# Edge layers of a graph network: adding the gates in the gathers instead of on the vector engine

## The reference, cut to what matters

```
ea = silu(edge_attr @ We + be)              # the gates, once: 100000 x 128
for l in range(4):
    msg = relu(x[src] + ea)                 # gather a row for each edge, add its gate, clip at zero
    agg = segment_sum(msg, dst, num_segments=n)
    h = x + agg
    h = silu(h @ W1[l] + b1[l]) @ W2[l] + b2[l]
    y = x + h
    x = layernorm(y) * gamma[l] + beta[l]
```

## Time and profile before

| | |
|---|---|
| median of 3 runs | 9549.08 us (9542.76 to 9550.45) |
| the profiled execution, its own time | 9545.06 us |
| its span, first to last instruction | 9543.3 us |
| GpSimd busy | 6696.7 us, 70% |
| TensorE busy | 4661.5 us, 49% |
| VectorE busy | 4305.5 us, 45% |
| ScalarE busy | 529.1 us, 6% |
| granted TensorE clock, mean | 0.61 of full speed |
| DMA | 960.76 MB, 101 GB/s over the span |

### The profile page before, as it was taken

How to read it: one execution, slowest core, us unless ns; L and a number is a source line. 1 busy time by engine, 2 the same in 40 slices (tenths; PEclk the granted TensorE clock), 3 DMA queues, 4 the chain that set the end, 5 groups by cost and what they waited for, 6 DMA issues and landing times.

```text
span 9543.3 us, 143586 instructions
## 1 busy us (share of the span) xinstructions
PE 4661.5 (49%) x19975; PEld 3800.2 (40%) x19976; DVE 4305.5 (45%) x9490; ACT 529.1 (6%) x1108; POOL 6696.7 (70%) x6591
## 2 busy tenths in 40 slices
PE   2766735544455344544445444453455444544455
PEld 1444424433344333433334333343444334443444
DVE  3455565654566445654456445672223223332222
ACT  1222211100000000000000000000000000000000
POOL 1777626557777677767777677776777677767776
PEclk9577768865566556565556555665555555555566
DMA  3998854223333333333333333331222222222222
GB/s 102 262 271 263 249 153 128 83 77 98 99 101 101 88 98 102 100 89 98 98 100 101 87 97 99 99 90 45 54 54 57 51 53 56 55 51 53 54 58 53
DMA packets 907432, 960.76 MB, mean 101 GB/s; under 512 B 442719, under 2 KB 610042, under 8 KB 906872
## 3 DMA queue, kind: packets, MB, share of 16 engines
q0 software_dynamic: 213248, 462.82, 18.9%
q1 hardware_dynamic: 572380, 399.74, 15.4%
q10 hardware_dynamic: 121756, 97.77, 3.1%
HBM read 801.39 MB, written 164.71 MB: 101 GB/s over the span
## 4 chain that ended last, share of the span: by engine, by line
POOL 55%; issue 21%; DMA 9%; DVE 6%; PE 4%; DVEq 2%; POOLq 1%; ACTq 1%; SPq 1%; ACT 0%
POOL rows L693 52%; DMA gates_by_edge<-gate 7%; PE ps_seg L823 2%; POOL msg L713 1%; POOL sums L693 1%; POOLq L324 1%; DVE msg L1452 1%; PE ps_mm L847 1%; DMA rows<-node_rows,idx 0%; DMA kv_rows<-gate 0%; PE ps_big L878 0%; PE ps_t L835 0%; ACTq L368 0%; DVE group_stats L1355 0%; DVEq L1288 0%
## 5 line engine op out<-in xcount | busy, mean ns | idle before, releaser
L693 POOL DMA_INDIRECT rows<-node_rows,idx x5488 | 5573.0, 1015 | 1919.1 <-issue 1669.6
L823 PE MATMUL ps_seg<-msg,onehot 128*128 128x128 f32 (+1 forms) x9800 | 2142.0, 387 | 2553.1 <-DVE sums L1309 2274.6
L823 PEld LDWEIGHTS ps_seg<-msg,onehot 128*128 128x128 f32 x9800 | 1838.0, 279 | 2854.2 <-DVE sums L1309 2535.0
L1288 DVE SCALAR_TENSOR_TENSOR onehot<-iota_f,win_base,dst_ch 128x512 f32<-128x512 f32 x1968 | 1512.9, 769 | 3200.4 <-PE ps_seg L823 2554.6
L823 PE MATMUL ps_seg<-rows,onehot 128*128 x5880 | 1393.7, 417 | 1559.9 <-SPq L590 1450.7
L823 PEld LDWEIGHTS ps_seg<-rows,onehot 128*128 128x128 f32 x5880 | 1220.9, 310 | 1729.8 <-issue 1728.2
L1452 DVE TENSOR_TENSOR msg<-q_res,rows 128x512 f32 (+1 forms) x984 | 677.1, 688 | 1108.8 <-SPq L590 1108.7
L693 POOL DMA_INDIRECT sums<-kv_rows,idx x784 | 773.4, 987 | 288.2 <-issue 230.0
L713 POOL TENSOR_TENSOR msg<-rows,score 128x512 f32 x245 | 325.4, 1330 | 420.6 <-SPq L590 197.0
L1309 DVE TENSOR_TENSOR sums<-sums,ps_seg 128x128 f32 (+1 forms) x1952 | 550.9, 282 | 0.1
L796 PE MATMUL ps_mm<-w_edge,attr_t 65*128 65x512 f32 x488 | 377.8, 867 | 195.0 <-ACT attr_t L949 191.0
(11 more groups left out here) (189 smaller groups left out, 1923.8 us busy)
## 6 DMA issues: line engine op xcount, KB each, us to landing
q_res<-gates_by_edge SPq DMA_DIRECT2D x784, 256.0 KB
rows<-node_rows,idx POOLq DMA_INDIRECT x5488
gates_by_edge<-gate ACTq DMA_DIRECT2D x244, 256.0 KB
rows<-dst_padded SPq DMA_DIRECT2D x196, 256.0 KB, 4.9
value_rows_by_edge<-sums SPq DMA_DIRECT2D x196, 256.0 KB
rows<-value_rows_by_edge SPq DMA_DIRECT2D x196, 256.0 KB, 2.6
idx<-src_padded SPq DMA_DIRECT2D x1568, 2.0 KB
node_rows<-h_res ACTq DMA_DIRECT2D x49, 448.0 KB
```

The source lines that it names most:

```text
L693: pool.indirect_dma_start(target[:, r, j, :], None, table, bass.IndirectOffsetOnAxis(ap=idx[:, r, j:j + 1], axis=0)).then_inc(rows_landed[ ...
L823: last = nc.tensor.matmul(ps_seg[u][:, 0:width], onehot[:, u, j, :], rhs(j), start=j == 0, stop=j == J - 1)
L1288: V.scalar_tensor_tensor(onehot[:, u, :, :], iota_f[:, :].rearrange("p (a n) -> p a n", a=1).to_broadcast([P, J, P]), win_base[:, ds(w, 1) ...
```

## The change

The gates of a chunk are loaded straight into the chunk's ring slot, and the four gathers add the rows to them (`compute_op=ALU.add`: the transfer reads the row and what stands in the slot, and writes the sum). GpSimd waits for the gates of the slot ahead of the gathers; SyncE no longer waits for them. VectorE takes one operation of the slot and a broadcast zero, a maximum, in place of the addition and the maximum. Its counter `msg_ready` now also does what `gates_added` did, and the seven slots for the gates go. The other passes gather as before.

```diff
-        gates = q_res[:, :, :].rearrange("p w d -> p (w d)")[:, 0:RING * J * D]\
-            .rearrange("p (s j d) -> p s j d", s=RING, j=J)
...
                     if kind == "edges":
-                        sp.dma_start(gates[:, r, :, :], gate_d[ds(c, 1)].rearrange("c p (j d) -> p (c j) d", d=D))\
+                        sp.dma_start(ring[:, r, :, :], gate_d[ds(c, 1)].rearrange("c p (j d) -> p (c j) d", d=D))\
                             .then_inc(gates_landed[r], 16)
...
-                    if kind == "edges":
-                        sp.wait_ge(gates_landed[r], (gates_before + turn + 1) * 16)
                     sp.sem_inc(rows_ready, 1)
...
-                chunk_pass(k, "edges", gates_added, l * N_ONEHOT, l & 1, also=lambda: layer_loads(l))
-            sp.wait_ge(gates_added, LAYERS * N_ONEHOT)
+                chunk_pass(k, "edges", msg_ready, l * N_ONEHOT, l & 1, also=lambda: layer_loads(l))
+            sp.wait_ge(msg_ready, LAYERS * N_ONEHOT)
...
-            def gather_pass(k, table):
+            def gather_pass(k, table, edges=False):
...
                 def body(c, r, turn):
                     pool.wait_ge(idx_loaded[r], (before + turn + 1) * 16)
                     wait_alone(pool, "pool", slot_free, before * RING + c + 1)
+                    if edges:
+                        wait_alone(pool, "pool", gates_landed[r], (gates_before + turn + 1) * 16)
                     for j in range(J):
                         pool.indirect_dma_start(
                             target[:, r, j, :], None, table,
-                            bass.IndirectOffsetOnAxis(ap=idx[:, r, j:j + 1], axis=0)).then_inc(rows_landed[r], 16)
+                            bass.IndirectOffsetOnAxis(ap=idx[:, r, j:j + 1], axis=0),
+                            compute_op=ALU.add if edges else ALU.bypass).then_inc(rows_landed[r], 16)
...
-                def add_gates(s, c, slot, u):
+                def relu(s, c, slot, u):
                     wait_alone(dve, "dve", rows_ready, c + k * CHUNKS + 1)
-                    V.tensor_tensor(msg[:, u, :, 0:D], gates[:, ds(slot, 1), :, :].rearrange("p s j d -> p (s j) d"),
-                                    ring[:, ds(slot, 1), :, :].rearrange("p s j d -> p (s j) d"), ALU.add)\
-                        .then_inc(gates_added, 1)
-                    dve.wait_ge(gates_added, l * N_ONEHOT + s + 1)
-                    V.tensor_scalar(msg[:, u, :, 0:D], msg[:, u, :, 0:D], 0.0, None, ALU.max).then_inc(msg_ready, 1)
+                    V.tensor_tensor(msg[:, u, :, 0:D], ring[:, ds(slot, 1), :, :].rearrange("p s j d -> p (s j) d"),
+                                    zero_col[:, :].rearrange("p (a b) -> p a b", a=1).to_broadcast([P, J, D]), ALU.max)\
+                        .then_inc(msg_ready, 1)
```

More of the change, by code:

```diff
@@ L282, in build_program @@
         agg_cleared = sem("agg_cleared")
-        gates_added = sem("gates_added")
         msg_ready = sem("msg_ready")
@@ L532, in chunk_pass @@
                 before = 0 if kind == "scores" else (k - 1) * (CHUNKS // slots)
-                gates_before = (k - L1_PASS) * (CHUNKS // slots)
                 def load_idx(c, r):
@@ L681, in _ @@
                     pool.sem_inc(batches_moved, 1)
-            def gather_pass(k, table):
+            def gather_pass(k, table, edges=False):
+                gates_before = (k - L1_PASS) * (CHUNKS // RING)
                 first = isinstance(k, int) and k == 0
@@ L725, in _ @@
             with pool.Fori(0, LAYERS) as l:
-                gather_pass(l + L1_PASS, tables)
+                gather_pass(l + L1_PASS, tables, edges=True)
             for n in range(3):
@@ L1446, in finish_layer @@
                     dve.sem_inc(group_done, 1)
-                def add_gates(s, c, slot, u):
+                def relu(s, c, slot, u):
                     wait_alone(dve, "dve", rows_ready, c + k * CHUNKS + 1)
-                    V.tensor_tensor(msg[:, u, :, 0:D], gates[:, ds(slot, 1), :, :].rearrange("p s j d -> p (s j) d"),
-                                    ring[:, ds(slot, 1), :, :].rearrange("p s j d -> p (s j) d"), ALU.add)\
-                        .then_inc(gates_added, 1)
-                    dve.wait_ge(gates_added, l * N_ONEHOT + s + 1)
-                    V.tensor_scalar(msg[:, u, :, 0:D], msg[:, u, :, 0:D], 0.0, None, ALU.max).then_inc(msg_ready, 1)
+                    V.tensor_tensor(msg[:, u, :, 0:D], ring[:, ds(slot, 1), :, :].rearrange("p s j d -> p (s j) d"),
+                                    zero_col[:, :].rearrange("p (a b) -> p a b", a=1).to_broadcast([P, J, D]), ALU.max)\
+                        .then_inc(msg_ready, 1)
                 begin_pass(k)
-                wait_alone(dve, "dve", gates_added, l * N_ONEHOT)
-                add_gates(0, 0, 0, 0)
+                wait_alone(dve, "dve", msg_ready, l * N_ONEHOT)
+                relu(0, 0, 0, 0)
                 def edge_layer(s, u, turn, row):
                     mark_next(k, s, u, row)
-                    add_gates(s + 1, row.get(CHUNK_, CHUNKS - 1, 1), row.get(SLOT_, RING - 1, 1), 1 - u)
+                    relu(s + 1, row.get(CHUNK_, CHUNKS - 1, 1), row.get(SLOT_, RING - 1, 1), 1 - u)
                     if not is_first(s):
```

## The result

| | before | changed |
|---|---|---|
| median | 9547.56 us (4 runs, 9542.76 to 9550.45) | 11197.86 us (4 runs, 11177.9 to 11205.49) |
| ratio of the times | 1 | 1.1725, 95% interval 1.171 to 1.174 |
| profiled execution: its time, span | 9545.06, 9543.3 us | 11177.9, 11176.1 us |
| GpSimd busy | 6696.7 us | 8359.2 us |
| VectorE busy | 4305.5 us | 3864.7 us |

The change costs 17%. The direction was forecast, the size was not: 10216 us, a loss of 7%.

What follows compares the result with a forecast made beforehand. GpSimd's back-to-back indirect gathers were taken as the bound. Terms of 659 + 9 + 1 - 4 + 2 + 0 = +667 us on 9545.06 us gave 10212, forecast as a median of 10216 us, range 9440 to 11400.

Steps and rivals of the forecast that it cites:

- the price of the adding gather: Edge-layer gathers on GpSimd: the adding form costs 0.21 us more each, 3136 times, +659 us.
- the ceiling: Upper end for an adding gather's extra time: the whole gather behind its first 0.11 us again, 0.83 us, 2603 us in all.
- 8 for the rest: Gate waits at layer starts +9, after the last layer's group update +1, layer ends -4, later landing of rows +2 us.
- The stalls: Edge-layer gathers held up by VectorE operations, 109 ns each, 342 us: taken as unchanged, 0, between -273 and +273 us.
- the faster rival: Edge-layer gathers: adding costs GpSimd nothing and a shorter VectorE step cuts stalls by 90 us, 9467 us; chance 0.33.
- The first gather's wait for gates: At each layer's start the first gather begins about 2.2 us later, waiting for gates: +9 us over four layers.
- The end of a layer: Last five VectorE steps of a layer, without the separate relu, save 0.1 to 0.43 us each: -4 us over four layers.
- The wait behind the last layer's group update: After a group update of the last layer, gates issued late delay their gather: +1.2 us, once.
- Price nil and faster: Edge-layer gathers: adding costs GpSimd nothing and stalls shrink by 90 us, with +8 at boundaries, 9467 us; chance 0.33.
- The transfer engines become the bound: Edge-layer gathers: adding costs the transfer engines six times as much, +1660 us, 11210 us; chance 0.08.
- The list writing is done again: Edge-layer gathers on GpSimd: everything behind a gather's start doubles, +0.83 us each, +2600 us, 12150 us; chance 0.07.
- The 423 us: Up to 984 x 0.43 us gained by removing VectorE's relu, if it locks GpSimd out for its whole length.

Runs made afterwards that it cites:

- e5: Changed kernel with plain gathers in the edge layers, overwriting the gates in the slot: 9471.89 us beside 9540.53 for the kernel before, 0.9925.
- e6: Kernel before with the iota row that the one-hot operation reads placed in PSUM: 9372.81 us beside 9540.53, 0.9822.
- e11: Kernel of e5 with the relu as an operation of one tile and a constant: 11345.7 us beside 11285.43 for the kernel before.

## Why the prediction was right and wrong

**The bound** was right: GpSimd issues without a pause, and every ns of a gather came through 3136 times. The gaps stayed 0.30 us, the new wait as an instruction cost nothing, and the convolutions' gathers stayed as they were (median 944 ns).

**The step that failed** is the price of the adding gather, in the prediction "one list would be 0.42 us ... I take half of it, 0.21 us". It measured 0.605 us: 1897 us and not 659. The picture behind it, time for each transfer written down, was the wrong one too: about 430 of the 603 ns are there whatever the number of rows. Its row, 946 against 944 ns for rows twice as long, varied the bytes; nothing in the trace varied the form of the instruction, and I let a row that is silent on the question pull the estimate down to a quarter of the ceiling. The measured price is 73% of that ceiling. What GpSimd does in the 430 ns stays open.

**The sum.** Forecast: 659 for the price, 0 for the stalls, 8 for the rest. Measured: 1897, -235 and -31, together the 1633 us by which the span grew, but for 2 us of rounding. That the time still lies under the upper end of the range, 11400 us, is luck: 0.605 us is above the 0.6 at which the forecast's own range ended, and the price alone would have given 9549 + 1897 = 11446 us.

**The stalls** I took as unchanged (0, bounds -273 and +273); they fell by 235 us. I had half of the mechanism in the faster rival, VectorE's shorter step, and left it out of the sum. By itself it takes 21 ns a gather off (before against e5), 66 us. The other half, that a slower gather begins less often while VectorE works, I had not considered; with the shorter step it takes another 54 ns (e5 against changed), 169 us.

**The boundaries.** The first gather's wait for gates was forecast at +2.2 us a layer, measured +2.7. The end of a layer, forecast at -1, measured -4.6, and behind the fourth layer, which had no term, -13.1. The forecast counted five steps of VectorE at the end; the backlog that the shorter step leaves is smaller as a whole. The wait behind the last layer's group update did not appear, and not in e5 either, where the gathers are as fast as before.

**The rivals.** "Price nil and faster", 0.33, fell; e5 is what it would have been, and its 9467 us stand beside 9472 measured. The condition wasn't met, and that the two agree is partly luck: the rival had 90 us of stalls less and 8 more at the boundaries, e5 has gathers shorter by 55 us and boundaries that are shorter, not longer. "The transfer engines become the bound" gave 11210 us, within 12 us of the result, and is wrong all the same: the rows land in time, and the gaps on GpSimd are the ones from before. The packets of one row did come, and a gather takes the transfer engines twice as long, 0.56 us and not 0.28. That is the factor of two which the prediction said the extra read asks for, and with the gates' 0.23 us it is far from the 1.85 us of a gather and its gap. "The list writing is done again" (12150 us) was nearest in mechanism, since the time is spent on GpSimd itself, but halving the rows took off a seventh of the price (603 to 516 ns) and not half.

By the Trainium skill ("Collectives: The Full Stack", Part 3, why ReduceScatter is half of AllGather) an add needs a second source read for every piece. On the transfer engines this case's traces agree: 0.56 us a gather for 0.28, though the packets also changed from 16 to 128, and no run here parts the two. Of GpSimd's time it could explain the 1.36 ns a row at most. And of the Trainium skill's "SBUF — State Buffer", "Who interferes with whom", I wrote that the row showed none of the lock of a two-port operation. e6 shows it where the gather *starts* inside the relu (1.19 us), and the earlier trace rows had it only in the middle of a gather, where it costs nothing. The trace of before has it too: 60 gathers begin inside the relu. With more than 0.2 us of it left, the 36 that begin in its first 0.04 us are not held up, and 16 of the 19 that begin later are. That agrees with this page of the Trainium skill, by which whoever issues first has the shared ports, and my reading of one row was too broad. The 423 us that I worked out by that rule were never there to gain: the gathers that begin inside the relu are longer by 3 us in all in the trace of before.

## What to carry to other kernels

Before work is moved into the DMAs of an engine, ask who issues them and whether that engine is the one that never waits: VectorE had 1068 us to spare here, GpSimd none, and the change took 441 us of busy time off the first at the price of 1663 on the second. Where the trace doesn't show a form of instruction, its price can be anything up to the ceiling: take the forecast from the middle of that span and not from a row that varies something else, or measure the form by itself with one edited argument. And where a gather-issuing GpSimd is the bound, look at which operands VectorE reads at the moment when a gather starts: moving one small constant into PSUM was worth 1.8%.

## What the runs showed of the hardware that I had not expected

- An indirect gather of 128 rows that adds costs GpSimd 1549 ns and not 944. Some 430 ns of the difference don't depend on the rows (worked out from 128 and 64 rows, plain and adding); the adding form still takes 1307 ns at 16 rows and 1329 at 8. It goes out as 128 packets of 512 bytes instead of 16 of 4096 and takes the transfer engines 0.56 us and not 0.28.
- A gather is held up when it begins while the one-hot operation or the addition runs on VectorE, which have two inputs in SBUF, or the relu, which has one. It is then longer by what is left of that operation less about 0.12 us (the median of 404 gathers in the addition of before, and of 179 in the relu of e6, with more than 0.2 us left). It is not held up when it begins in the operation's first 0.04 us (the relu of before, 36 of 36), and the addition of before adds nothing where it begins in the middle of a gather (339 gathers, at most 956 ns). Where e11's one-input maximum does, 139 gathers are longer by 11 ns in the mean and by 0.12 us at most.
- With one of two inputs in PSUM an operation doesn't hold a gather up: 731 gathers in the one-hot operation of e6 took at most 957 ns, and 294 in the sum's addition (L1309) of before at most 948. GpSimd's own two-input multiplication ran in 1059 and not 1330 ns in e6.
- VectorE read an operand of the one-hot operation from PSUM in the same 751 ns as from SBUF (753).
